# Edge attention with its softmax weights in PSUM beside the sums

## The reference, cut to what matters

```
scores = einsum('ehd,egd->ehg', Q[src], K[tgt]) / sqrt(64)    # 4 x 4 numbers per edge
attn   = softmax(scores, axis=-1)
msg    = einsum('ehg,egd->ehd', attn, V[tgt])
proj   = (msg + Ee[et]) @ Wo.T + bo
hidden = segment_sum(proj, src)                               # summed per source node
```

## Time and profile before

| what | us |
|---|---|
| median of 3 runs without profiler | 7309.79 |
| fastest and slowest of them | 7300.85 and 7316.3 |
| span of the profiled execution | 9062.1 |

### The profile page before, as it was taken

The page is one execution under the profiler, slowest core; times in us unless marked ns, Lnnn a source line. Parts: engine busy times, 40 slices in busy tenths (PEclk is TensorE's granted clock), DMA queues, the critical chain, the costliest instruction groups (busy, mean ns, idle before and its releaser), DMA issues. The chain is left out here.

```text
span 9062.1 us, 179398 instructions
## 1 busy us (share of the span) xinstructions
PE 4683.8 (52%) x60555; PEld 3816.1 (42%) x60555; DVE 5139.2 (57%) x12108; ACT 1224.9 (14%) x2828; POOL 4305.5 (48%) x3974
## 2 busy tenths in 40 slices
PE   0000000488732555476766767766676777445552
PEld 0000000366621444356666556666566665323331
DVE  7996000377754444655665455555455555557767
ACT  0000000122201111111111011111011111122220
POOL 5887777200063555135655055554255552066640
PEclk9999999999955555689999889898889988755555
DMA  0000000000012333155552255551355540133320
GB/s 24 3 1 1 1 1 1 1 0 0 4 26 65 101 101 101 48 167 156 158 157 62 88 147 161 152 150 31 117 154 158 156 120 21 30 94 98 98 75 24
DMA packets 708570, 691.60 MB, mean 76 GB/s; under 512 B 234981, under 2 KB 589355, under 8 KB 708165
## 3 DMA queue, kind: packets, MB, share of 16 engines
q0 software_dynamic: 227328, 446.06, 18.1%
q1 hardware_dynamic: 480846, 240.51, 9.6%
HBM read 766.03 MB, written 77.58 MB: 93 GB/s over the span
## 5 line engine op out<-in xcount | busy, mean ns | idle before, releaser
L1669 POOL DMA_INDIRECT kvring<-kvtab,oth x1776 | 1834.4, 1033 | 1619.5 <-PE ea_psg L1731 923.2
L1069 POOL DMA_INDIRECT e_hg<-htab,oth_d x992 | 991.8, 1000 | 1130.9 <-issue 713.4
L1720 PE MATMUL ea_pss<-ea_qb,ea_kT 128*128 128x128 f32 x7104 | 1198.0, 306 | 0.0
L1720 PEld LDWEIGHTS ea_pss<-ea_qb,ea_kT 128*128 128x128 f32 x7104 | 1113.8, 224 | 32.3
L1790 DVE TENSOR_TENSOR acc<-ea_psg,acc 128x64 f32 x1776 | 399.0, 225 | 1161.3 <-remote 1049.8
L1731 PE MATMUL ea_psg<-ea_mix,kvring 128*64 128x64 f32 x14208 | 581.9, 240 | 887.6 <-DVE ea_mix L1832 877.2
L1731 PEld LDWEIGHTS ea_psg<-ea_mix,kvring 128*64 128x64 f32 x14208 | 522.1, 152 | 984.8 <-issue 691.2
L255 POOL DMA_INDIRECT sb_rec<-srawrec,splacei x392 | 430.9, 1099 | 960.5 <-PEq L56 815.9
L1196 PE MATMUL e_psg<-e_Em,e_hg 128*32 128x32 f32 x15872 | 569.9, 245 | 439.6 <-issue 399.4
L1764 ACT ACTIVATE ea_kT<-ea_pst 128x512 f32<-128x512 f32 x888 | 481.9, 595 | 2201.5 <-remote 1331.3
L1196 PEld LDWEIGHTS e_psg<-e_Em,e_hg 128*32 128x32 f32 x15872 | 439.2, 146 | 622.0 <-issue 524.2
(11 more groups left out here) (506 smaller groups left out, 8250.9 us busy)
## 6 DMA issues: line engine op xcount, KB each, us to landing
ea_qb<-qtab SPq DMA_DIRECT2D x1776, 64.0 KB
qtab<-at_qst SPq DMA_DIRECT2D x75, 512.0 KB, 3.3
kvring<-kvtab,oth POOLq DMA_INDIRECT x1776
e_stack<-ohtab SPq DMA_DIRECT2D x744, 32.0 KB
kvtab<-at_kvst SPq DMA_DIRECT2D x75, 256.0 KB, 2.7
e_hg<-htab,oth_d POOLq DMA_INDIRECT x992
ea_mk<-mtab SPq DMA_DIRECT2D x444, 3.0 KB
htab<-Hd SPq DMA_DIRECT2D x2, 3200.0 KB, 11.6
```

The costliest lines, as they stand in the source:

```text
L1069: pool.indirect_dma_start(out=hg[:, b % RING, u, :], out_offset=None, in_=htab, in_offset=bass.IndirectOffsetOnAxis(ap=oth[:, b * 4 + u:b ...
L1669: pool.indirect_dma_start(out=kv[:, b % R, u, :], out_offset=None, in_=kvtab, in_offset=bass.IndirectOffsetOnAxis(ap=oth[:, b * QB + u:b * ...
L1720: mm = pe.matmul(ps_s[r % 2][:, u, k * 2 * HN:(k + 1) * 2 * HN], kT[:, r % 2, u, k, :], qb[:, r, u, :], start=False, stop=True, skip_group ...
```

## The change

The weights of a batch are no longer written to the SBUF tile `att`, which goes away, but to PSUM. The two tiles of sums grow from [128, 4, 64] to [128, 8, 64], that is to the whole of bank 6 and of bank 7. Their first four rows are the sums as before. The fifth row, 64 numbers, is the place of the weights of a batch (4 tiles of 16); the other three are not used. The weights have two buffers now, since the two sums have. The instruction that makes the weights keeps its inputs and writes to PSUM; the mixing product reads `hot` from SBUF as before and the weights from PSUM.

```
-        sc, ex, att = sb("sc", [P, QB, G, G]), sb("ex", [P, QB, G, G]), sb("att", [P, QB, G, G])
+        sc, ex = sb("sc", [P, QB, G, G]), sb("ex", [P, QB, G, G])
...
-        ps_g = [pb(f"psg{i}", [P, QB, HN]) for i in range(2)]
+        sums = [pb(f"psg{i}", [P, 2 * QB, HN]) for i in range(2)]
+        ps_g = [bank[:, 0:QB] for bank in sums]
+        ps_w = [bank[:, QB, :].rearrange("p (u q) -> p u q", u=QB) for bank in sums]
...
-                    dve.tensor_tensor(att[:, :, :, :], ex[:, :, :, :], tot[:, :, :].unsqueeze(2).broadcast_to([P, QB, G, G]),
+                    dve.tensor_tensor(ps_w[r % 2].rearrange("p u (g h) -> p u g h", g=G), ex[:, :, :, :], tot[:, :, :].unsqueeze(2).broadcast_to([P, QB, G, G]),
                                       ALU.mult).then_inc(s["att"], 1)
...
                     dve.tensor_tensor(mix[:, r % 2], hot[:, bass.ds(b * QB, QB), :].unsqueeze(2)
                                       .broadcast_to([P, QB, G * G, NBS]),
-                                      att[:, :, :, :].rearrange("p u g h -> p u (g h)").unsqueeze(3)
+                                      ps_w[r % 2].unsqueeze(3)
                                       .broadcast_to([P, QB, G * G, NBS]), ALU.mult).then_inc(s["mix"], 1)
```

## The result

The changed kernel takes 7119.55 us in the median of 4 runs (7115.22 to 7123.17), the kernel before 7307.07 us in 4 runs beside them. The ratio is 0.9743, with a 95% interval of 0.9729 to 0.9757: 187.5 us faster, 2.6%. That lies inside the range and on the side that was forecast, but it is more than twice the 84 us of the sum, near rival B's 7100 us.

The account below looks back on a forecast made before the run. The late semaphore was taken to bound the profiled loop, and POOL's 5.2 us a batch where that wait is shorter. Prices 1 to 3 were 0 and the ended hold 84 us: 7310 - 84 = 7226 us, range 7050 to 7345 us.

Parts of the forecast that it names:

- the sum: Whole kernel: 7310 us less 84 us for gathers no longer held gives 7226 us, 1.2% faster.
- rival B: POOL bounds the unprofiled loop and the hold falls on every batch: 207 us and up, 7100 or 7050 us; chance 0.17.
- What bounds the loop: Passes: late semaphore bounds the profiled 7.00 us batch; elsewhere POOL's 5.2 us does, above DVE's 4.45 us.
- Prices 1 and 2: Mixing product reading weights from PSUM, and the weights being written there: each 0 us; reading at most 93 us.
- Rival C: Mixing product reading weights by a step of zero from PSUM is longer: 7357 us at half its upper bound; chance 0.14.
- Price 3: PE and DVE sharing banks 6 and 7 for weights and sums: 0 us.
- Price 4: Gathers starting beside the mixing product are held while both its operands are in SBUF; ending this gains 84 us.
- the ring: Ring of four batches, places freed by `agg`: claimed to take up part of the hold; no size of its own.
- the lower end: Least gain from unheld gathers, from their mean above the median without those behind `hot`: 0 to 34 us.
- The upper end: Gathers back to back every 1.30 us: one held in 85% of batches for 0.55 us, 207 us in all.
- A: Rival: the hold is hidden in POOL's 923 us wait for `agg`, nothing is won, 7310 us within 15; chance 0.24.
- The profiled span: Span of the changed kernel's profiled execution, expected at 9025 to 9060 us against 9062.1 us before.

Follow-up runs that it names:

- experiment 6: Changed kernel with the gather of every batch's fourth tile left out, that tile computed from zeros: 6850.48 us, ratio 0.9385.
- experiment 5: Kernel before with the gather of every batch's fourth tile left out, that tile computed from zeros: 6851.47 us, ratio 0.939.
- experiments 7: Changed kernel with the 16-place row copied to PSUM, so the product making `hot` has one operand in SBUF: 7080.44 us, ratio 0.9699.
- 8: Changed kernel plus an unread DVE product of 256 numbers a batch, both operands in SBUF: 7127.93 us, ratio 0.9764.
- 9: Changed kernel plus an unread DVE product of 256 numbers a batch, one operand in PSUM: 7115.6 us, ratio 0.9748.
- experiment 1: Kernel before, unchanged, profiled a second time: 7301.75 us in this run.

## Why the prediction was right in its mechanism and wrong in its size

**What bounds the loop.** The prediction put the unprofiled loop "closer to POOL's 5.2 us than to 7.00". Right: 5.61 us before, which is 5.19 us and a hold of 0.42 us. DVE's chain was estimated at 4.45 us and is 4.61. That is still 0.58 us under POOL's floor.

**Prices 1 and 2, the reading and writing of PSUM, set at nothing.** Right. The product takes 1222 ns against 1226, and the chain 4.607 us against 4.611. The writing of the weights rose from 215 ns in the second profile of before to 223 ns (medians):

```profile
L1827 DVE TENSOR_TENSOR ea_att<-ea_ex,ea_tot x444: 215/215/269, 2954.8 to 5944.5; 128x64 f32<-128x64 f32 x148
```

The cover of 0.22 us behind the fourth `take` hides these 8 ns. The estimated 65 ns a batch worked out from the Trainium skill ("VectorE: DVE Perf Modes", section "The TRN2 errata — SBUF-src ops pay a fixed extra latency per instruction") do not appear for a product with one operand in each memory. Had they, experiment 6 would be slower than 5 by an estimated 444 x 0.065 = 29 us; the two are within 1.0 us. Rival C falls with it.

**Price 3, the shared banks.** No cost shows: PE is busy 1995.5 us in the windows after, 2010.4 before, and the chain of experiment 6 is no longer than that of 5.

**Price 4, the operand that leaves SBUF.** The mechanism was right: experiments 7, 8 and 9 switch the hold on and off by the place of one operand (in 7 with a copy of 0.18 us a pass beside it). The Trainium skill has the lock behind it ("SBUF — State Buffer", section "🔬 SBUF: two separate sides"): a DVE instruction with two SBUF inputs and a GpSimd instruction that reads SBUF shut each other out of a shared pair of ports. The trace agrees for a gather that starts inside the product (1.32 and 1.63 us, ending 0.87 and 0.86 us behind it). It does not show the other half, that an operation which started first shuts out the second for its whole length: the product that starts 0.53 us into a gather takes 1.23 us as ever, and in the second profile of before the 350 products that start while a gather is under way take 1226 ns in the mean.

**The step that failed is the size of that term.** The prediction took 84 us, "half way on a scale of ratios between 34 and 207 us", "because POOL's 5.2 us and DVE's 4.45 us are near each other and the ring of four batches takes up part of the hold". Measured are 187 us, or 0.42 us a batch. The 84 us give the lower end as much weight as the upper, and the lower end was no bound. Its 34 us were read from a loop of 7.00 us, where a gather started inside the product in only 48 of 444 batches; in the second profile of the same kernel one does in 417, and there the held time is 1776 x (1119 - 998) ns = 215 us, less 28 us behind `hot`, 187 us. So the 34 us told of that execution and not of the kernel. The upper end, "with gathers back to back", follows from what the prediction itself had said of POOL as the bound, and it was near: 0.47 us a batch against 0.42. Counted over the single gathers of the second profile, 326 are held, in 73% of batches and for 0.57 us each, where the prediction had 85% and 0.55. Nor does the ring take anything up: the idle time before the gathers is 822.1 us in the second profile of before and 821.4 us after the change, so the whole hold stood on top of it. A ring evens out a delay of one gather only if POOL can catch up later, and as the bound of this loop it can't. Experiments 5 and 6 show the case where it can, and there the hold costs nothing.

**Rivals.** B was right in its regime ("POOL is the bound without the profiler"), though not in holding "on every batch". A's evidence, the 923 us wait for `agg`, was that of the stretched execution; without it the wait is 120.4 us.

**The profiled span.** "9025 to 9060 us" was far off, since the stretching did not come with profiling as such: nine later profiles and that of the changed kernel are as long as their runs. Of the 1762 us between the two profiles of before, 3109.1 - 2473.3 = 636 us lie in the windows of the three passes, where the prediction took "a good part" of its 1752 us to be.

## What to carry to other kernels

When POOL issues indirect DMAs back to back, look for DVE instructions with both operands in SBUF beside them, and give one operand a place in an unused part of a PSUM bank; the longer the instruction, the more it is worth (here 11 us for a product of 256 numbers and 187 us for one of 1024). Ask first whether POOL is the bound there: if it is, every held microsecond counts; if it waits for something else, a hold only shortens that wait, as the 305 us of experiment 5 did. And before waits are sized from a profile, compare its span with the unprofiled time; where they differ by a fifth, bounds read from the waits, or from how often two engines meet, are bounds on that execution alone.

## What was not expected of the hardware

One profiled execution of the kernel before was 24% longer than its runs (9062.1 us), and in it DVE's `take`s waited for steps of PE's semaphore, up to 4.4 us each, that the profile ties to no product. The next profile of the same kernel had a span of 7300.0 us and no such wait for "remote" in front of the `take`s, only the 531.5 us for PE's products. TensorE's granted clock differed too: 0.92 of its full 2.4 GHz in the first window of the earlier trace rows, and 1.00 in the same window of the second profile (the third number from the end of the row):

```profile
2955.10:3775.10 820.00, 668.44 (x8793) 592.60 (x8791) 610.98 (x1617) 180.41 (x439) 633.62 (x577) 1.00 0.60 169
```

What made the first one slow stays open.

A held gather does not lose its start: it ends 0.87 us, not 1.00, behind the product, and a gather that is under way when the product begins neither waits nor lengthens it (3302.63 and 3303.16 in experiment 1). The first moments count as well: in that profile the 14 gathers that start within 0.04 us behind a product's start take 1.00 us, and those that start 0.05 to 0.10 us behind it take 2.00 to 2.05 us.

Not tried is the same change in `segment_sums`, where the earlier trace rows show a gather of 1.90 us beside a product of two SBUF operands.
